# Linear attention in one unrolled sequence of chunks, with the output's transposes, its root and its addition moved in the step

## The reference, cut to what matters

```
q, k, v = causal depthwise convolutions (4 taps) of x @ Wq, x @ Wk, x @ Wv
z = x @ Wz;  beta = sigmoid(x @ Wb);  g = -exp(A_log) * softplus(x @ Wa + dt_bias)
per chunk of 128 tokens, with E[i,j] = exp(sum of g from j+1 to i):
    T = inverse of (I + strictly lower part of beta * (k k^T) * E)
    u = T (v - decay * k S) * beta
    o = decay * q S + lower part of (q k^T * E) u
    S = decay_of_the_chunk * S + k^T (u * decay_to_the_end)
y = o / sqrt(mean(o^2) + eps) * norm_w * silu(z)
X += y @ W_out          (summed over the heads)
```

## Time and profile before

| what | value |
|---|---|
| median of 3 runs | 11030.72 us (10996.83 to 11032.3) |
| profiled execution, its own time | 11019.79 us |
| its span on the core | 11017.7 us |
| granted TensorE clock, mean over the span | 0.824 |
| PE busy in the span | 8421.8 us (76%) |
| DVE, ACT, POOL busy | 6391.6, 4265.4, 3195.2 us |
| instructions | 282876 |

### The profile page before, as it was taken

The page is one execution under the profiler, slowest core; times in us unless marked ns, Lnnn a source line. Parts: engine busy times, 40 slices in busy tenths (PEclk is TensorE's granted clock), DMA queues, the critical chain, the costliest instruction groups (busy, mean ns, idle before and its releaser), DMA issues. The chain is left out here.

```text
span 11017.7 us, 282876 instructions
## 1 busy us (share of the span) xinstructions
PE 8421.8 (76%) x119656; PEld 6032.2 (55%) x119656; DVE 6391.6 (58%) x11875; ACT 4265.4 (39%) x7157; POOL 3195.2 (29%) x2445
## 2 busy tenths in 40 slices
PE   7996788888887888878888787887785565564457
PEld 3444666666765665656566565665454464453222
DVE  6662466666566767757677575775674434434443
ACT  3552333333334656656566565663221111111110
POOL 0110122222223646636366363660001121120000
PEclk8995788888888999989999898998896676675555
DMA  0000000000001212212122121220000000000000
GB/s 11 1 1 1 3 4 4 4 4 4 4 4 40 67 41 69 64 45 65 48 62 65 45 64 46 64 67 0 12 0 3 0 0 0 0 0 1 0 2 8
DMA packets 189934, 254.44 MB, mean 23 GB/s; under 512 B 58038, under 2 KB 84373, under 8 KB 187926
## 3 DMA queue, kind: packets, MB, share of 16 engines
q1 hardware_dynamic: 188822, 237.65, 8.2%
HBM read 27.80 MB, written 2.10 MB: 3 GB/s over the span
## 5 line engine op out<-in xcount | busy, mean ns | idle before, releaser
L1735 PE MATMUL wa_front<-w_wqkv,wa_xsT 128*128 128x512 f32 x2400 | 1229.4, 637 | 184.8 <-issue 137.4
L1657 POOL TENSOR_TENSOR XNT<-XNT 128x1024 f32<-128x1024 f32 x396 | 937.0, 2366 | 303.4 <-DVE XNT L1841 303.4
L1660 POOL TENSOR_TENSOR XNT<-XNT,wa_rnorm 128x1024 f32<-128x1024 f32 x396 | 753.3, 1902 | 440.5 <-DVE wa_rnorm L1849 440.5
L1838 DVE TENSOR_TENSOR XNT<-wa_front,w_scaled 128x1024 f32<-128x1024 f32 x396 | 473.4, 1195 | 473.3 <-ACT wa_sq L1676 301.7
L1735 PEld LDWEIGHTS wa_front<-w_wqkv,wa_xsT 128*128 128x128 f32 x2400 | 425.4, 198 | 539.4 <-issue 515.6
L1676 ACT ACTIVATE wa_sq<-wa_front 128x1024 f32<-128x1024 f32 x402 | 408.5, 1016 | 279.6 <-PE wa_front L1735 279.6
L1841 DVE TENSOR_TENSOR XNT<-wa_front,w_scaled 128x512 f32<-128x512 f32 x792 | 505.4, 679 | 0.0
L2514 POOL COPY a3d_k<-a3x_qk 128x128 f32 x32 | 9.3, 290 | 1688.6 <-SPq L2511 1688.6
L1854 DVE TENSOR_REDUCE wa_norm<-wa_sq 128x16 f32<-128x1024 f32 x396 | 478.5, 1208 | 0.0
L2538 ACT ACTIVATE a3d_Zt<-a3d_big 128x512 f32<-128x512 f32 x192 | 114.6, 597 | 886.3 <-PE a3d_big L2544 886.3
L446 PE MATMUL a0h_ring<-a0h_QT,a0h_KT 32*128 32x512 f32 (+3 forms) x1536 | 442.9, 548 | 14.4 <-ACT a0h_E L564 10.4
(11 more groups left out here) (554 smaller groups left out, 20908.2 us busy)
## 6 DMA issues: line engine op xcount, KB each, us to landing
wa_v_look<-wa_v_all SPq DMA_DIRECT2D x1188, 128.0 KB, 2.3
wa_v_look<-wa_v_all SPq DMA_DIRECT2D x792, 64.0 KB, 2.0
w_wqkv<-in_L_ffn_Wqkv_dram SPq DMA_DIRECT2D x6, 1024.0 KB
w_wo<-in_L_ffn_Wo_dram SPq DMA_DIRECT2D x6, 512.0 KB
w_wqkv<-in_L_ffn_Wqkv_dram SPq DMA_DIRECT2D x12, 256.0 KB
f2w_raw<-in_L_ffn_w_dram SPq DMA_DIRECT2D x48, 64.0 KB, 1.9
out_dram<-X SPq DMA_DIRECT2D x1, 2048.0 KB, 8.7
w_w<-in_L_ffn_W_dram SPq DMA_DIRECT2D x6, 341.0 KB
```

The lines of the kernel that those rows point to most:

```text
L1657: g.tensor_tensor(rot[:, at], rot[:, at], part[:, at], ALU.add).then_inc(s[summed], 1)
L1660: g.tensor_tensor(rot[:, at], rot[:, at], spread(rnorm[:, at, :], HDW), ALU.mult).then_inc(s[done], 1)
L1735: last = pe.matmul(front[:, first + i, :], xsT[:, slot, :], wqkv[:, (2 * n + i) * 512:(2 * n + i + 1) * 512], start=True, stop=True)
L1838: v.tensor_tensor(rot[:, n], src, cos, ALU.mult)
```

## The change

The loop over heads is gone. One stage a1s is unrolled over 64 chunks (8 heads times 8 chunks) in 67 steps; a chunk t belongs to head t // 8. The weights and taps get two slots, and the next head's weights are loaded by SP without a stage of their own, turned by PE at the ends of the steps with s % 8 = 5 and 6 (into bank 2), and scaled and copied by ACT there. S and the history are cleared in the pipeline at a head's last chunk. Inside the step, the transposes of y move to the next step, between k S and q S; the output product moves behind zt(0) and the K projection; the square root moves to the middle of the step, ahead of evict_z(4) and the exponential E; the addition to X moves ahead of u; and y and its reciprocal move behind the gate and the last square of XT.

```
-        with nc.Fori(0, H) as h:
-            with Stage(nc, "a1h") as st:
...
-            with Stage(nc, "a1s") as st:
-                delta_chunk_steps(nc, st, X, xnt4, c, w, taps, S, hist, gh, bh, nb, XT, T64, xs, eps, small)
+        with Stage(nc, "a1s") as st:
+            delta_chunk_steps(nc, st, X, xnt4, c, d, w, raw_w, taps, half_norm, S, hist, g_all, beta_all, nb_all, XT, T64, xs,
+                              eps, small)
...
+    CHUNKS = HEADS1 * BLOCKS
+        return tuple(step - n if 0 <= step - n < CHUNKS else None for n in range(4))
+    steps = CHUNKS + 3
...
+        @block.sync
+        def _(sp):
+            for n in range(HEADS1):
+                if n >= 1:
+                    sp.wait_ge(s["w_ps"], 2 * n)
+                if n >= 2:
+                    sp.wait_ge(s["conv_ready"], 2 * BLOCKS * (n - 1))
+                (eight dma_start as in a1h)
...
+            def turn_weights(n, part):          # PE
+                if part == 0:
+                    pe.wait_ge(s["loaded"], 8 * 16 * (n + 1))
+                else:
+                    pe.wait_ge(s["w_ready"], 2 * n + 1)
+                    pe.wait_ge(s["scaled"], n + 1)
+                for k, m in enumerate((0, 1, 3, 4) if part == 0 else (2, 5, 6, 7)):
+                    last = pe.transpose(bank[2][:, k, :], raw_w[:, m, :], c.ident)
+                last.then_inc(s["w_ps"], 1)
...
                     four_of(bank[5], lambda b: conv[:, r % 3, K, b, :], lambda b: S[:, b, :], s["kS_ps"])
+                if e is not None:
+                    pe.wait_ge(s["y_ready"], e + 1)
+                    pe.wait_ge(s["E_ready"], min(step, CHUNKS))
+                    turn_four(bank[7], y, s["yT_ps"])
                     four_of(bank[6], lambda b: conv[:, r % 3, QC, b, :], lambda b: S[:, b, :], s["qS_ps"])
...
                     turn_four(bank[3], conv[:, q % 3, K], s["ktok_ps"])
-                if e is not None:
-                    four_of(bank[4], lambda b: yT[:, b, :], lambda b: w[:, 3, :], s["out_ps"])
                 zt(0)
                 (K projection)
+                if e is not None:
+                    pe.wait_ge(s["yT_ready"], e + 1)
+                    four_of(bank[4], lambda b: yT[:, b, :], lambda b: weights(e)[:, OUT_W, :], s["out_ps"])
...
+                if r is not None and r % BLOCKS < BLOCKS - 1:
                     four_of(bank[6], lambda b: ktok[:, r % 2, b, :], lambda b: uend[:, b, :], s["s_ps"])
...
-                if r is not None:
-                    pe.wait_ge(s["y_ready"], r + 1)
-                    turn_four(bank[7], y, s["yT_ps"])
                 if q is not None:
                     tx(6)
+                turn_weights(next_head(step, 5), 0)
+                turn_weights(next_head(step, 6), 1)
...
+            def keep_weights(n, part):          # ACT, at the ends of the same steps
+                if part == 0:
+                    (four scalings of raw_w by taps, ACT.Copy with a scale)
+                    (after w_ps:) a.activation(into[:, 0:3, :], bank[2][:, 0:3, :], ACT.Copy)
+                    a.activation(into[:, OUT_W, :], bank[2][:, 3, :], ACT.Copy, scale=half_norm[:, 1:2])
+                else:
+                    a.activation(into[:, V_W:V_W + TAPS, :], bank[2][:], ACT.Copy)
...
                     last.then_inc(s["Nc_ready"], 1)
+                if e is not None:
+                    a.wait_ge(s["yT_ps"], e + 1)
+                    a.activation(yT[:], bank[7][:], ACT.Copy).then_inc(s["yT_ready"], 1)
...
                 evict_z(3)
+                if r is not None:
+                    a.wait_ge(s["msq_ready"], r + 1)
+                    a.activation(std[:], msq[:], ACT.Sqrt, scale=1.0 / P, bias=eps[:]).then_inc(s["std_ready"], 1)
+                evict_z(4)
                 if j is not None:
                     a.activation(E[:], bank[7][:], ACT.Exp).then_inc(s["E_ready"], 1)
-                evict_z(4)
...
-                (std behind tanh; yT behind evict_z(6))
...
+                if e is not None:                # DVE, ahead of u
+                    v.wait_ge(s["out_ps"], e + 1)
+                    v.tensor_tensor(mine, bank[4][:], mine, ALU.add).then_inc(s["added"], 1)
                 if r is not None:
                     v.wait_ge(s["u_ps"], r + 1)
                     v.tensor_tensor(u[:], bank[7][:], beta, ALU.mult).then_inc(s["u_ready"], 1)
...
-                (rstd and y ahead of the gate)
                     (gate)
                     v.tensor_copy(XT[0:64, slot, :, 64:P], bank[4][0:64, :, 0:64]).then_inc(s["x6_ready"], 1)
+                if r is not None:
+                    v.wait_ge(s["std_ready"], r + 1)
+                    chain(v.reciprocal(rstd[:], std[:]))
+                    v.tensor_tensor(y[:], y[:], spread(rstd[:], P), ALU.mult).then_inc(s["y_ready"], 1)
```

More of the change, by code:

```diff
@@ L1011, in delta_chunk_steps @@
                 "gatez_ready qk_ps AT_ready kS_ps qS_ps qS_used R_ready u_ps u_ready uend_ready o_ps o_done s_ps "
-                "newS_ready s_used msq_ready std_ready y_ready yT_ps yT_ready out_ps added chain")
+                "loaded scaled w_ps w_ready newS_ready s_used msq_ready std_ready y_ready yT_ps yT_ready out_ps added chain")
     K, T0 = 0, TAPS - 1
@@ L1084, in tx @@
                             pe.wait_ge(s["x6_ready"], q)
+                        if n == 1 and step % BLOCKS in (6, 7) and step // BLOCKS + 1 < HEADS1:
+                            pe.wait_ge(s["w_ready"], 2 * (step // BLOCKS + 1) + step % BLOCKS - 5)
                         if n == 1 and e is not None:
@@ L1114, in vtok_part @@
                     for n in range(TAPS):
-                        last = pe.matmul(bank[3][:, b, :], xs[:, q % 2, b, n:n + P], w[:, 4 + n, :], start=(n == 0),
+                        last = pe.matmul(bank[3][:, b, :], xs[:, q % 2, b, n:n + P], weights(q)[:, V_W + n, :], start=(n == 0),
                                          stop=(n == TAPS - 1))
@@ L1139, in _ @@
                     turn_four(bank[3], conv[:, q % 3, K], s["ktok_ps"])
+                zt(0)
+                if j is not None:
+                    pe.wait_ge(s["xs_ready"], j + 1)
+                    pe.wait_ge(s["w_ready"], 2 * (j // BLOCKS) + 2)
+                    if q is not None:
+                        pe.wait_ge(s["N_ready"], q + 1)
+                    pe.matmul(flat(bank[0][:]), weights(j)[:, K_W, :], xs[:, j % 2, :, T0:], start=True,
+                              stop=True).then_inc(s["raw_ps"], 1)
                 if e is not None:
@@ L1162, in _ @@
                         pe.wait_ge(s["ktok_ready"], q + 1)
-                    pe.matmul(flat(bank[3][:]), w[:, 0, :], xs[:, j % 2, :, T0:], start=True,
+                    pe.matmul(flat(bank[3][:]), weights(j)[:, Q_W, :], xs[:, j % 2, :, T0:], start=True,
                               stop=True).then_inc(s["raw_ps"], 1)
@@ L1294, in _ @@
                                  ACT.Exp).then_inc(s["decays_ready"], 1)
+                keep_weights(next_head(step, 5), 0)
+                keep_weights(next_head(step, 6), 1)
         @block.gpsimd
@@ L1443, in _ @@
                     v.tensor_tensor(AT[:, slot], bank[0][:], Eincl[:], ALU.mult).then_inc(s["AT_ready"], 1)
-                if r is not None:
-                    v.wait_ge(s["std_ready"], r + 1)
-                    chain(v.reciprocal(rstd[:], std[:]))
-                    v.tensor_tensor(y[:], y[:], spread(rstd[:], P), ALU.mult).then_inc(s["y_ready"], 1)
                 if q is not None:
```

124 lines of the change are left out of this document (80 added, 44 removed).

## The result

| | before | changed |
|---|---|---|
| median | 11026.17 us (4 runs) | 10513.95 us (4 runs, 10505.34 to 10521.09) |
| ratio | | 0.954, 95% interval 0.9521 to 0.9559 |
| profiled execution's span | 11017.7 us | 10503.5 us |
| mean granted clock over the span | 0.824 | 0.843 |
| the linear attention, from its first load of weights to its last addition (before: to the end of the loop, 0.7 us later) | 2240.7 us | 1708.7 us |

A forecast was written before the change was run, and what follows sets the result against it. PE sets the pace, with waits for y and the addition and a slow clock. Fill 71.0, 61 steps of 26.6 (1622.6), drain 40.4 and weights 3.1 give 1737.1 for 2240.7 us, so 10527 us; range 10480 to 10710.

The forecast's parts named there:

- The boundaries and fills: Seven inner boundaries and fills between heads go by unrolling: 207 us less if steps stay at 31.4 us.
- The step: N to N in the unrolled stage: 26.6 us, between 26.2 (chain hidden) and 26.9 (chain all slow).
- The clock: PE from transposes of y to zt(0): slow clock costs 0.7 us per step and goes with the long idle.
- What brings the clock down: The low clock on PE comes only behind the 2.55 us idle; the 1.36 us idle before tx(1) brings none.
- The transposes: Moved on PE after Gram and k S of the next step: takes away the 2.55 us wait for y per step.
- The addition: To X, ahead of u on DVE: fits in the wait for u, so tx(1) loses its 1.36 us.
- The root: On ACT in mid-step, both table loads hidden by 1.4 and 0.7 us: cost nothing, else up to 2.6 us a step.
- The weights: PE's added transposes at step ends for 7 heads, 6.2 us in all: cost 3.1 us.
- (b): Rival: ACT's mid-step table loads not hidden, up to 2.6 us a step; step 29.2, 10686 us; chance 0.10.
- (d): Rival: instruction supply to PE slows the unrolled steps; at 37 us a step 11161 us; chance 0.03.
- (c): Rival: PE's two waits return elsewhere, only unrolling pays; step 29.5 to 31.4, 10704 to 10820 us; chance 0.12.
- (a): Rival: the clock still drops in each step; step 27.3 to 28.8, 10570 to 10661 us; chance 0.20.

The follow-up runs named there:

- e1: Changed kernel with the step's old order (transposes of y and root at the end, addition after o), so unrolling alone: 10863.28 us, ratio 0.9848.
- e7: Changed kernel with y and its reciprocal behind N on DVE and the transposes of y behind q S on PE: 10449.13 us, ratio 0.9479.
- e5: e1 with two unread products of four added on PE while it waits for y: 10702.4 us, ratio 0.9707.
- e8: e2 with one unread product of four added on PE ahead of its wait for y: 10493.91 us, ratio 0.9526.
- e2: Changed kernel with transposes of y back ahead of tx(6), y ahead of the gate, output product ahead of zt(0): 10628.35 us, ratio 0.9626.
- e4: Changed kernel with the root back at the step's end ahead of evict_z(6), E ahead of evict_z(4): 10656.5 us, ratio 0.9656.
- e3: Changed kernel with only the addition to X put back after o: 10613.63 us, ratio 0.9618.
- e9: Changed kernel with the root at the step's end behind evict_z(6), E ahead of evict_z(4): 10514.62 us, ratio 0.9538.

## Why the prediction was right

10514 us against a forecast of 10527, and the stage 1708.7 us against 1737. The course was the one forecast: the boundaries go, both waits go, the wait for lev takes their place. The sizes were off both ways. The unrolling gave 182 us instead of 207, and the moves on top of it 350 (e1's stage less the changed kernel's) instead of 296, as the slow clock was priced too low. That the total came within 13 us, when the stage missed by 28, is luck: in the two profiled executions what lies outside the stage took 18 us longer in the changed kernel.

- *The boundaries and fills.* Forecast 207 us at an unchanged step; e1 shows 182. I took 31.4 from the last four full steps of head 0 and left out its first, which is 33.8 long; over all forty the step is 31.82, and 61 times the difference is 26 us.
- *The step.* Forecast 26.6, between PE's own work (26.2) and the chain of y, N and lev (26.4 to 26.9). It is 26.23, set by that chain, as the wait for lev shows. With y and lev both slow, as they are (1325 and 862 ns), I had worked that chain out at 26.9. It is shorter because PE reaches tx(6) at 20.71 after zt(0) (2020.53 to 2041.24) and not at 20.9, and above all because the square of XT starts 0.71 us after tx(6) (at 2041.95) and not the 1.01 that I took from the slow stretch of the earlier trace rows. PE's own work was mis-sized: without the wait it is 25.3 us, as e7 shows. The causes are in the timeline above. The eight matmuls of tx(6) take 0.61 us to the next start where I took 0.97; Gram, k S and q S take 0.99, 0.97 and 0.90, where I took 1.09 for each from another product; the transposes of y take 0.49 instead of 0.59.
- *The clock.* This is the term that was mis-sized, and it is the same error seen from the other side. I read 0.7 us of slow clock off the step of the earlier trace rows, because I held its slow stretch against these too long durations. The 0.97 of tx(6), which I called the upper level, was itself taken at 1906.82, in that slow stretch. This row of the kernel before shows the clock at 0.50 there:

```profile
1907.00:1909.00 2.00, 2.00 (x14) 1.88 (x14) 0.42 (x1) 1.97 (x3) 0.00 (x0) 0.50 0.00 0
```

  Against e5's rows that step loses 6.97 - 5.40 = 1.57 us, and the mean step, which is 1 us longer than that one, loses more: e5 gives 2.19 us, and e8 against e2 gives 28.32 - 26.31 = 2.0 us though e8 has a product more for its idle. This is the largest gain of the moves after the wait for y. In e1 the step's 31.81 us are 25.3 of work, 2.53 and 1.36 of waits, some 0.2 of small ones, and 2.4 of clock (what is left).
- *What brings the clock down.* I wrote that it follows only the long idle. That step failed: 0.84 us ahead of the transposes (e2) and 1.33 us ahead of tx(6) (e4) did it as well, while 1.36 us ahead of tx(1) plus 0.81 ahead of zt(0) (e3) did not. The rule of the Trainium skill that I had set against my term (TensorE: Matmul & The Clock Gate, "A second HAM failure mode: psum-queue depth-cycling"), that short recurring idles can keep the clock moving, agrees with e2 and e4. The changed kernel does not show it: its 0.80 us in each step leave the clock at 1.00. It has its short idle in another place; that was luck of the order, not something I had derived.
- *The transposes.* I gave their move the whole wait of 2.55 us. With the root in mid-step and the transposes in their old place, 0.84 are left (e2); with the transposes moved and the root late, behind evict_z(6), the step is 26.34 (e9). Either removes the long wait. Without added products, the rest of the wait and the slow clock behind it went only in orders with the transposes moved.
- *The addition.* 1.36 us forecast, 1.59 measured (e3).
- *The root.* Costed at nothing, with 1.4 and 0.7 us of margin. The margins are 1.36 and 0.63, and e9 confirms the nothing.
- *The weights.* Nothing of them is seen in the steps in which they are turned: there the wait for lev is 0.66 us instead of 0.85, and from tx(6) to zt(0) it is 5.47 us with the added transposes (1962.62 to 1968.09) as without (2041.24 to 2046.71). I had put 3.1 us for them in all.
- *The rivals.* (b) is out by ACT's rows. PE does wait for Zt seven times, 4.3 us in all, but e1, with its root at the step's end, has the same 4.3 us; the first three lie in steps in which S is cleared and the state's update is left out. (d) is out as PE's waits for "issue" are 2.6 us in all. (c) took place in its mildest form, the wait for lev. (a) did not occur, though e2 and e4 are two small changes of the order from which it does.

## What to carry to other kernels

A wait of PE has two prices, the time it stands still and the clock of what follows, and the second can be the larger; it can be measured by letting PE do useless matmuls there. When a wait is removed, read which chain is next before settling the new order: here two instructions in DVE's list, y and N, stood the wrong way round for another 50 us. Durations for PE's list are best taken from the place where the operation stands and at the upper clock, since products of four of one size took 0.90 to 1.09 us by place. When two engines slow each other, as DVE and POOL did here, look for the order in which the loss falls on an instruction that nobody waits for.

## What was not expected of the hardware

The granted clock fell to 0.50 (1.2 GHz) behind an idle of 0.84 us at the step's end and stayed at 1.00 (2.4 GHz) behind one of 1.36 us in its first half. In e5, 0.65 us of idle at the same place as in e2, behind two added products, left it up. So neither the length of an idle nor its place alone decides; what does, within the lists of these kernels, stays open. In a step of e2, the one before the stretch shown above, the clock was still at 1.00 when PE started again (2000.92) and fell about 1 us later, while PE was busy:

```profile
2001.00:2001.50 0.50, 0.50 (x4) 0.34 (x4) 0.47 (x1) 0.00 (x0) 0.50 (x2) 1.00 0.00 0
...
2002.50:2003.00 0.50, 0.50 (x3) 0.50 (x4) 0.29 (x1) 0.00 (x0) 0.00 (x0) 0.50 0.00 0
```

And the same instructions outside the stage took between 8771 and 8802 us in thirteen profiled executions. These 31 us are half a microsecond for each of 61 steps, so orders whose steps differ by less are told apart by the stage's own rows and not by the total of one execution.
